# DLRM tower on one core: gathers grouped by sixteen throughout, and a new written-out order of the work

## The reference

```python
e = jnp.stack([tbl_0[ids[:, 0]], ..., tbl_31[ids[:, 31]]], axis=1)       # 2048 x 32 x 64
z = jnp.einsum('bpe,fpe,bpf->bp', e[:, row_idx, :], L0_rec_kernel, e[:, col_idx, :])   # 2048 x 496
h = jnp.concatenate([z, dense_ctx], axis=1)                              # 2048 x 512
h = jnp.maximum(h @ W_top1 + b_top1, 0.0)                                # 512
h = jnp.maximum(h @ W_top2 + b_top2, 0.0)                                # 256
y = h @ W_top3                                                           # 1
```

## Time and profile before

| what | value |
|---|---|
| time, median of 3 runs | 840.17 us (839.22 to 840.34) |
| the profiled execution's own time | 839.88 us |
| its span, first to last instruction | 838.1 us |
| TensorE busy | 753.0 us (90%) |
| VectorE busy | 651.5 us (78%) |
| ScalarE busy | 644.2 us (77%) |
| GpSimd busy | 484.0 us (58%) |
| mean granted TensorE clock | 0.976 of full speed |

### The profile page before, as it was taken

The page is one execution under the profiler, slowest core; times in us unless marked ns, Lnnn a source line. Parts: engine busy times, 40 slices in busy tenths (PEclk is TensorE's granted clock), DMA queues, the critical chain, the costliest instruction groups (busy, mean ns, idle before and its releaser), DMA issues.

```text
span 838.1 us, 16496 instructions
## 1 busy us (share of the span) xinstructions
PE 753.0 (90%) x4672; PEld 305.5 (36%) x4672; DVE 651.5 (78%) x601; ACT 644.2 (77%) x5196; POOL 484.0 (58%) x518
## 2 busy tenths in 40 slices
PE   0498969889898999999947998999999999999998
PEld 0244545355533333333312233333343333333333
DVE  0388969779677878999946896898978999789950
ACT  0279988967649728899953698799786999999952
POOL 6776776767676776666666766666766666000000
PEclk9999999999999999999979998999999999999999
DMA  9611111211212121111212121121122112000100
GB/s 335 204 40 38 40 38 25 52 25 38 51 27 50 26 51 25 32 42 23 51 24 50 25 48 24 24 50 25 25 50 41 31 24 51 1 2 1 27 1 0
DMA packets 34644, 36.40 MB, mean 43 GB/s; under 512 B 18676, under 2 KB 20980, under 8 KB 34424
## 3 DMA queue, kind: packets, MB, share of 16 engines
q0 software_dynamic: 16384, 16.81, 11.0%
q1 hardware_dynamic: 18168, 18.53, 7.6%
HBM read 26.91 MB, written 0.01 MB: 32 GB/s over the span
## 4 chain that ended last, share of the span: by engine, by line
PE 48%; POOL 31%; issue 11%; DMA 9%; DVE 0%; DVEq 0%; ACT 0%; POOLq 0%
POOL rows L407 21%; PE y_ps L507 15%; PE y_ps L529 11%; POOL kept_rows L407 10%; PE sum_ps L543 9%; DMA rows<-tbl_dram,idx 7%; PE layer_ps L559 3%; DMA kept_rows<-tbl_dram,idx 2%; PE layer_ps L562 2%; PE y_ps L465 1%; PE y_ps L576 1%; PE y_ps L522 1%; PE y_ps L585 1%; PE y_ps L510 1%; PE y_ps L580 0%
## 5 line engine op out<-in xcount | busy, mean ns | idle before, releaser
L669 ACT ACTIVATE batch_products<-batch_products 128x64 f32<-128x64 f32 x2576 | 615.4, 242 | 105.5 <-DVE batch_products L763 105.3
L669 ACT ACTIVATION_READ_ACCUMULATOR batch_products<-batch_products 128x1 f32 x2576 | 486.4, 189 | 0.0
L407 POOL DMA_INDIRECT rows<-tbl_dram,idx x384 | 362.4, 944 | 168.9 <-issue 102.1
L752 DVE TENSOR_TENSOR products<-y_ps,xt 128x1024 f32<-128x1024 f32 (+1 forms) x224 | 255.5, 1197 | 44.2 <-PE y_ps L508 38.5
L763 DVE TENSOR_TENSOR batch_products<-y_ps,kept_rows 128x1024 f32<-128x1024 f32 x192 | 225.1, 1216 | 24.7 <-PE y_ps L531 16.7
L507 PE MATMUL y_ps<-xt,kernel_sb 64*128 64x512 f32 (+1 forms) x448 | 207.8, 598 | 0.4 <-DVE products L752 0.3
L508 PE MATMUL y_ps<-xt,kernel_sb 64*128 64x512 f32 (+1 forms) x448 | 207.8, 598 | 0.0
L529 PE MATMUL y_ps<-kernel_sb,xt 64*128 64x512 f32 x384 | 196.1, 639 | 4.8 <-DVE products L744 2.5
L531 PE MATMUL y_ps<-kernel_sb,xt 64*128 64x512 f32 x384 | 196.1, 639 | 0.0
L543 PE MATMUL sum_ps<-products,selector 128*32 128x512 f32 (+1 forms) x1520 | 155.9, 523 | 4.2 <-ACT z_sb L639 1.7
L407 POOL DMA_INDIRECT kept_rows<-tbl_dram,idx x128 | 120.9, 945 | 57.3 <-issue 35.5
(11 more groups left out here) (54 smaller groups left out, 408.7 us busy)
## 6 DMA issues: line engine op xcount, KB each, us to landing
kernel_sb<-pair_kernel_dram SPq DMA_DIRECT2D x15, 512.0 KB, 11.2
rows<-tbl_dram,idx POOLq DMA_INDIRECT x384, 2.5
special<-xt SPq DMA_DIRECT2D x48, 128.0 KB
kept_rows<-tbl_dram,idx POOLq DMA_INDIRECT x128, 2.5
special<-xt SPq DMA_DIRECT2D x32, 64.0 KB
w_sb<-w_dram SPq DMA_DIRECT2D x1, 1024.0 KB
w_sb<-w_dram SPq DMA_DIRECT2D x1, 512.0 KB
kernel_sb<-pair_kernel_dram SPq DMA_DIRECT2D x1, 256.0 KB, 3.1
```

The source lines that it names most:

```text
L407: pool.indirect_dma_start(rows_of(g, q, t)[:, h, :], None, tables[j], bass.IndirectOffsetOnAxis(ap=idx[:, n, j:j + 1], axis=0)).then_inc(l ...
L669: last = nc.scalar.activation(product, product, ACT.Copy, accum_out=batch_sums(unit)[:, column:column + 1])
L752: nc.vector.tensor_tensor(into[:, :, 0:size], y[:, :, 0:size], by, ALU.mult).then_inc(unit_done, 1)
```

## The change

`opens_flight` is made the same for all whole chunks: two pairs, so sixteen gathers, between two waits. That changes segments 3 and 4 only. `BURSTS` is replaced by another list of words. The number of duos, quads, batches, sums, layer steps and mixes stays as it was; the 80 pairs to turn are the same too, but fewer of them are turned two at a time, so there are 72 turn steps where there were 58. The diff, with the first words of each list:

```diff
-    "050201 300000 120400 310000 210300 420200 500100 220500 400100 300203 400100 400200 460501 300200",
...
-    "411300 411430 402300 401410 413300 401300 401400 411100 402400 400000 502000 300000T",
+    "010001 000003 200201 210201 200200 000002 500100 000002 000100 400100 000101 500000 300301 100101 400202",
...
+    "300300 300100 200100 300320 400300 500000 300000T",
...
 def opens_flight(field):
     g, q, h = field
-    if half(g):
-        return h == 0 and q % 4 == 0
-    if chunk(g) == 1:
-        return h == 0 and q % 2 == 0
-    return h == 0
+    return h == 0 and q % (4 if half(g) else 2) == 0
```

## The result

| | before | changed |
|---|---|---|
| time, median | 839.86 us (839.22 to 840.34, 4 runs) | **818.87 us** (818.76 to 819.05, 4 runs) |
| span of the profiled execution | 838.1 us | 817.3 us |

The ratio is 0.9751, with a 95% interval of 0.9734 to 0.9768. The kernel is 21 us faster, a little under half of the 43 us that were forecast. In some of the later runs every kernel, the one before among them, took some 1.2 ms at a granted clock of 0.82 to 0.85; they stand under "Not settled", and nothing is concluded from them.

The account below looks back on a forecast made before the run. Gathers were taken to bound the kernel until 529 us, TensorE's own work after. Turn at 345.2 + 425.1 for the rest with friction + 24.8 last network + 1.8 around the span = 796.9 us, range 782 to 822.

Parts of the forecast that it names:

- What bounds the kernel now: Whole span: until 529 us TensorE keeps step with GpSimd's gathers, then works off the rest, busy 283.2 of 283.9 us.
- By my sum over the steps, TensorE reaches this turn within a us of the landing: Turn of pair 15, segment 2: reached at the landing, 345.2 us instead of 352.46, so 7.3 us gained.
- the early part doesn't catch up: Rival, chunk 0: VectorE's some 50 us against gathers' 49; lateness up to 10 us, so 807; no chance of its own.
- The work behind that turn: After pair 15, segment 2: priced TensorE work of 406.8 us against 421.6 in the old order, 14.8 less.
- Friction: Behind that turn: time over priced work, 4.5% against 1.8% before, with VectorE idle some 22 us at long layer runs.
- my case: The forecast's own case: friction 3 to 6% behind that turn, 790 to 803 us, chance 0.51.
- VectorE becomes the bound: Rival: layer-run starvation, short leads before readers and sums' waits for products add up to 9%, 815 us; chance 0.2.
- Do the gathers hold it?: Segment 3, pairs 7 and 9: gathers hold TensorE one us at most, no long wait, so no half clock.
- So much of the gain hangs on the groups of sixteen in this segment: Segment 3: without the removed landing waits, pair 9 would hold TensorE to 460.5, costing 8 us.
- Single turns: 14 more turn steps: 0.04 us each for VectorE, nothing for TensorE; possible waits for copies counted in the friction.
- slower rival: Behind each of 31 turns, TensorE waits for a copy; slower from 1.4 us a turn, 859 at 2 us; chance 0.04.
- What would show it: Signs: last gather 23 us earlier, pair 15, segment 2, turned at 345 to 347, clock 1.00, tail 415 to 435 us.

## Why the prediction was half right, step by step

The span went down by 838.1 - 817.3 = 20.8 us. By the prediction's own terms (us gained):

| term | forecast | measured |
|---|---|---|
| up to the turn of pair 15, segment 2 | +7.3 | -3.5 |
| less priced work behind it (a sum by prices, not measured) | +14.8 | +14.8 |
| waits, half clock and friction of before less friction after | +39.2 - 18.3 = +20.9 | 39.2 - 29.6 = +9.6 |
| last network | 0 | -0.1 |

- **What bounds the kernel now**: right. The part up to 529 us was held by gathers and the last one by TensorE's own work; halving VectorE's multiplications gave 1 us.
- **"By my sum over the steps, TensorE reaches this turn within a us of the landing"**: wrong by 10.8 us, and the first step that failed. The sum held TensorE's work against the gathers and left VectorE out. As a sum over TensorE alone it was right: with half the multiplications the turn stands at 345.2 in the new order and at 352.8 in the old one, so the finer order is worth the 7.3 us where VectorE keeps up. From the turn of pair 11, segment 0, to this turn VectorE is busy 53.9 + 74.8 + 122.6 = 251 us of 290, and can only work when TensorE has units for it. The rival "the early part doesn't catch up" named the mechanism, VectorE's 50 us beside gathers 49 us apart, and priced it at up to 10 us; I had it "in the range" with no chance of its own.
- **The work behind that turn**: right as a whole, by the 417.2 us of the run with half the multiplications. One price was short: a change of shape is paid again by the first unit behind it (below).
- **Friction, "I take 4.5%"**, the second step that failed: that VectorE costs TensorE more than the old 1.8% was right and the size was off: 29.6 us on 406.8, 7.3%, so 11.3 us more than the forecast's 18.3. The need of 371 us was right (375.5 busy), and so was the idle time at long layer runs: 22.7 us at the eight runs of four and 3.9 at the three of three, where some 22 in all were forecast. Of the 29.6 us, 19.2 go away with half of the multiplications. What was wrong is the price put on two engines this close: 4.5% was chosen between 1.8% and 9%, from no row. TensorE is not late at the layer runs, where VectorE idles, but in the long runs of units and at the sums behind them. The measured 7.3% lies between my case (3 to 6%) and the rival "VectorE becomes the bound" (9%, 815 us). With the early lateness on top, which that rival did not count, the kernel came out behind it.
- The Trainium skill, TensorEngine Tiling (Array Packing), PSUM Bottleneck, warns that emptying PSUM may become the bottleneck once TensorE is sped up; I gave it 0.2. The runs agree with it for the new order (29.4 us for half of the multiplications) and not for the old one (1 us). The engines' rates are the same in both, so they do not decide it. Up to 529 us the gathers held TensorE first in the old order; in its last stretch nothing else did, and VectorE still cost only 1.9 us.
- **"Do the gathers hold it?"** No, right. **"So much of the gain hangs on the groups of sixteen in this segment"**: wrong, they are worth nothing in the new order. Pair 9 of segment 3 was expected at its turn at 452.0 and came there at 465.7, with 10.8 us of early lateness and the friction since, so it was in time with groups of eight as well. A slack that was computed from a TensorE that is too fast turned a free thing into a needed one. Where VectorE was relieved, the pair came to its turn at 452.08 and waited 1.37 us for its gather, as the prediction had it.
- **Single turns**: the copy waited for is 1.3 us in the whole tail. The slower rival (1.4 us or more behind each of 31 turns) did not come.
- **What would show it**: the last gather 23.4 us earlier (686.69, before 710.06), the granted clock of 1.00 and no gather wait behind 346 came true. The turn at 345 to 347 and the tail of 415 to 435 us did not (356.0, 436.4), nor quite VectorE's 87% (375.5 of 436.4, 86%). "Wrong: that turn later than 352 (the early part)" is what happened.

## What to carry to other kernels

When a wait is removed, add up the second busiest engine over the same stretch as the first, against the same clock of gathers, and do so in every stretch, also where the first engine seems to have time to spare. Cheap test before any new order: halve the second engine's work and see whether the time moves; here it said 1 us for one order and 29 us for the other. The second engine's share of a stretch does not foretell its cost: at 86 to 87% it was 1.9 us of 284 in one order and 19.2 us of 436 in the other. Look at how its work lies, at the places where it is left idle for longer than its buffers last, and run the halved test on the new order before a percentage is put on it. Three new cuts of the same sequence got nothing back here.

## What the runs showed of the hardware

- **The first unit after 128-row steps is dearer.** The second record of a duo starts 0.42 or 0.43 us behind its first in a run (685.34 to 685.76), but 0.53 or 0.54 in the first one behind a sum (684.37 to 684.91). That comes on top of the 0.10 at the change itself, and half of VectorE's work does not take it away (3.5 us in both tails). Where it is paid in full, a change to 128 rows and back costs 0.3 us and not 0.2; over the tail it comes to 3.5 us for 58 such first units, 0.06 each.
- **With three buffers the slower engine's pace begins at the sixth unit of a run.** In the run shown the pitch is 0.86 us up to the fourth, 0.91 to the fifth, 1.13 to the sixth. Over the changed tail the mean is 0.87 from the third unit to the fourth, 0.91 to the fifth (41 cases) and 1.10 to the sixth (29), and 0.86 at all of these places with half of VectorE's multiplying. The first unit of a run has gone through VectorE 2.3 to 2.4 us after it started on TensorE (684.37, and VectorE's first multiplication of that run ends a quarter into 685.55 + 4.62); each further unit adds 0.27.
